# The next group's filter work spread over two superblocks, and its square root moved from ScalarE to three Newton steps on VectorE

## The chip, the cores and the metric

One core of a Trainium2 chip runs the whole program. The metric is the device time of one execution in microseconds (us); lower is better.

## What is computed

The input `x` is (8, 64, 56, 56) in float32. Four layers follow each other, each with its own group normalisation and a residual:

```
x = x + L0(gn(x))   # decoupled dynamic 3x3 filter
x = x + L1(gn(x))   # 1x1 convolution gated by a sigmoid
x = x + L2(gn(x))   # 3x3 convolution with ternary weights
x = x + L3(gn(x))   # attention over the 3136 pixels, softmax
```

The change touches what L0 needs before its taps. From the normalised image it makes two filters:

```
y  = relu(mean(x) @ w1.T + b1) @ w2.T + b2          # 9 taps per channel
cf = (y - mean) / (std(ddof=1) + 1e-10) * fn_std     # channel filter
sf = einsum(x, ws) + bs                              # 9 taps per pixel
sf = (sf - mean) / (std(ddof=1) + 1e-10) * gain      # spatial filter
out = sum over taps of patch * cf * sf
```

The standard deviation of `sf` needs one square root per pixel.

## The kernel before

**Groups and layers.** Two images make a group on the 128 partitions (64 channels each); there are 4 groups, three in a loop and the last written out after it. A group goes through L0, L1, L2 and L3 in order. A chunk is 448 pixels (8 rows), 7 chunks to an image.

**Attention.** L3 takes the queries in 7 superblocks of 448 columns, and the keys in 25 steps of 128 rows. In step j TensorE (PE) waits for the exponentials of step j (`exp_done`), multiplies them with the values (L1239, 4 matmuls), and makes the scores of step j+2 (L1195, 4 matmuls). ScalarE (ACT) takes the exponential of the scores of a step (L897) into one of 5 buffers, once GpSimd (POOL) has added the buffer of five steps before into its running sum (L1008). Superblocks 0 to 5 also find the maxima of the next superblock: 49 tiles, about two a step, made by PE (L1163) in PSUM banks 4, 5 and 7 in rotation and reduced by VectorE (DVE, L665); three rows of blocks of them are summed by ACT too (L854), two steps later. The tiles for the last superblock end at step 19 of superblock 5 (`SPLIT_STEP`), after which DVE splits the maxima (`split_max`) and PE and ACT move them into the query rows (L1188, L869). Superblock 6, the last, has no such tiles. A superblock's denominators (L1205, L1209) come at step 2 of the next one, the reciprocals (L701 to L705) on DVE at step 3, and POOL's two products of `finish` (L987, L989) after its step 8; after the last superblock they follow at once.

**The front.** What the next group's L0 needs before its taps is called the front. It reads `xin`, which the queue of SyncE has loaded again at the start of L3, and no DMA belongs to it. In groups 0 to 2 it is spread over the steps of superblock 6 by one function `front_at(j)` per engine; for group 0 it runs at the start of the program (the prologue), with no attention beside it. Its parts, by step:

- DVE: the statistics of the 7 chunks (`front_stats`, L468) at step 0, `squares` at 3, `var_eps` at 4, `front_bias` at 6, `front_mid` at 8, `front_sum_squares` (L538 to L542) at 15, `front_parts` (L546 to L562) at 18, `front_centre` (L514 to L523) at 19, `front_channel_filter` (L525 to L529) at 22.
- PE: the pair mean and pair variance (L1038, L1042) at 2 and 3, the small product of `front_mid` (L1047) at 7, the spatial filter (L1060, 8 matmuls for each of 7 chunks) at 8 to 14, the channel filter (L1052, 18 matmuls) at 16, and the transposes of the split filter (L1071) at 20, 20, 21, 22, 23, 24, 24.
- ACT: the normalisation of a chunk (L777) at 7 to 13, the square root (`front_root`, L795) after the exponential of step 16, and a copy of each transposed piece (L799) one step after its transpose, the last two behind the superblock.
- POOL: `power` (L954) before its step 5 and `channel_root` (L958) before its step 21.

Every engine takes its instructions in the order of the program, so a wait in one of these parts also holds what is behind it. `link` makes DVE wait for its own last result before the next instruction. The first tap of the next group (L1085) waits for all 7 copies, and the PE transposes wait for `front_parts`. The last denominators on PE wait for POOL's last sum.

`plan_banks` gives the maximum tiles, the max rows and the denominators their PSUM banks by estimated times. The front uses banks 4 and 5 (`FB`, `SFB`).

The square root and what follows it:

```python
nc.scalar.activation(sfs[:, 4, :], sfs[:, 2, :], ACT.Sqrt, scale=1.0 / (TAPS - 1))
# front_parts: one Newton step on it
s0 = s4 + 1e-30;  s1 = 1 / s0
s3 = (s2 * 0.5/(TAPS-1)) * s1
s5 = s4 * 0.5 + s3
```

Of the kernel before, what the change touches and what calls it, by code (L numbers as in the profile page):

```python
# [13 lines left out]
F32R = mybir.dt.float32r  # L14
BF16 = mybir.dt.bfloat16
# [11 lines left out]
NJ = HW // CH  # L27
# [29 lines left out]
FRONT_XN = 7  # L57
FRONT_SF = 8
FRONT_TR = (20, 20, 21, 22, 23, 24, 24)
FRONT_ROOT = 16  # L60
# [34 lines left out]
def plan_banks():  # L95

    tiles, rows, dens = {}, {}, {}
# [20 lines left out]
    for k in range(NQ * (NJ - 1)):  # L118
# [14 lines left out]
    return tiles, rows, dens  # L133


TILES_AT, ROWS_BANK, DEN_BANK = plan_banks()


# [30 lines left out]
def build(nc, x, weights, vectors, cst, out):  # L169
    with ExitStack() as ctx:  # L170
# [129 lines left out]
        sfvar_ready = sem("sfvar_ready")  # L300
        sfsd_ready = sem("sfsd_ready")
# [57 lines left out]
        FRONT_LINKS, LINKS = 23, 31  # L359
# [67 lines left out]
        def _(dve):  # L427
# [70 lines left out]
            def front_stats(g):  # L498
                n[0] = 0
                dve.wait_ge(x_loaded, 16 * g + 16)  # L500
                for i in range(NJ - 1):
                    chunk_stats(xin, i)
                mean_var(g, 0, chunk_stats(xin, NJ - 1))
# [32 lines left out]
            def front_sum_squares(g):  # L536
# [28 lines left out]
            def group(g, more):  # L565
# [142 lines left out]
                def front_at(j):  # L708

                    if j == 0:  # L710
# [666 lines left out]
```

## Time and profile before

| what | value |
|---|---|
| median of 3 runs | 1879.36 us (1878.1 to 1879.47) |
| the profiled execution | 1879.96 us |
| its span, first to last instruction | 1878.2 us |
| PE busy | 1646.5 us, 88% |
| DVE busy | 1258.0 us, 67% |
| ACT busy | 1249.8 us, 67% |
| POOL busy | 1099.3 us, 59% |

The span is from the first to the last instruction of the core; the execution is 1.76 us longer. A busy share is an average over stages with different limits. PE is the TensorE matmul and PEld its weight load. In a timeline row the first number is the start in us from the span's start, the second the time taken by all instructions of the row, `x` how many they are, and the bracket how long the engine had been idle before it and what ended that. An instruction that has started and has to wait for a port of the memory shows the wait in its duration.

### The profile page before, as it was taken

How to read it: one execution, taken by the hardware profiler on the slowest of the kernel's cores; microseconds unless marked ns; L12 is line 12 of the kernel's file. 1: busy time of each engine (PE TensorE's matmuls, PEld its weight loads, DVE VectorE, ACT ScalarE, POOL GpSimd, SP SyncE). 2: the span in 40 equal slices, each digit the busy share in tenths (PEclk: the TensorE clock that was granted, in tenths of full speed). 3: DMA queues.
4: the chain of work that ended last, by engine and by line, in shares of the span. 5: the costliest groups of instructions: out<-in, count | busy, mean ns of one | idle time of the engine just before them, and what ended most of it. 6: DMA issues, size and time to landing. Idle time of an engine off the chain costs nothing.

```text
span 1878.2 us, 35981 instructions
## 1 busy us (share of the span) xinstructions
PE 1646.5 (88%) x10840; PEld 826.0 (44%) x10840; DVE 1258.0 (67%) x2446; ACT 1249.8 (67%) x2324; POOL 1099.3 (59%) x898
## 2 busy tenths in 40 slices
PE   5887899999887699999988779999999787999997
PEld 4363344444436344444444534444454353444442
DVE  5947777775584777777467477777748657777760
ACT  2036788888412788888831278888872347888885
POOL 3610577778651067777855006777777402677777
PEclk9988899999889899999998889999999898999998
DMA  2004000000000400000000040000000011000000
GB/s 84 0 1 86 2 7 6 6 6 7 11 0 1 86 1 6 6 6 7 11 7 1 1 85 1 6 6 11 6 6 6 0 27 26 6 6 6 6 6 11
DMA packets 10104, 26.91 MB, mean 14 GB/s; under 512 B 2256, under 2 KB 6608, under 8 KB 9424
## 3 DMA queue, kind: packets, MB, share of 16 engines
q1 hardware_dynamic: 9936, 24.79, 5.5%
q8 instruction: 90, 1.47, 0.3%
q14 instruction: 78, 0.64, 0.1%
HBM read 8.73 MB, written 6.42 MB: 8 GB/s over the span
## 4 chain that ended last, share of the span: by engine, by line
PE 54%; issue 15%; DVE 12%; POOL 9%; ACT 9%; POOLq 1%; DVEq 0%; ACTq 0%
PE PS L1239 22%; PE PS L1163 11%; PE PS L1195 10%; DVE nmt L672 4%; ACT PS L854 3%; DVE nmt L665 2%; ACT Pb L897 2%; PE PS L1060 2%; POOL VT L970 2%; POOL VT L965 2%; PE PS L1135 2%; POOL VT L967 2%; POOL VT L974 1%; POOL accP L1008 1%; PE PS L1126 1%
## 5 line engine op out<-in xcount | busy, mean ns | idle before, releaser
L665 DVE TENSOR_REDUCE nmt<-PS 128x1 f32<-128x448 f32 x1176 | 680.3, 620 | 280.8 <-PE PS L1163 276.4
L1008 POOL TENSOR_TENSOR accP<-accP,Pb 128x512 f32<-128x512 f32 (+1 forms) x532 | 678.3, 1275 | 168.1 <-ACT Pb L897 144.6
L897 ACT ACTIVATE Pb<-PS 128x896 f32<-128x896 f32 (+1 forms) x700 | 638.9, 914 | 130.2 <-PE PS L1195 107.9
L1239 PE MATMUL PS<-Pb,VT 128*64 128x448 f32 x2800 | 656.0, 548 | 4.4 <-ACT Pb L897 3.6
L1163 PE MATMUL PS<-Ka,Qa 96*64 96x448 bf16 x2744 | 480.9, 362 | 55.9 <-DVE nmt L665 28.1
L1195 PE MATMUL PS<-Qa,Ka 99*64 99x448 bf16 x2744 | 489.8, 358 | 5.3 <-ACT Qa L869 4.0
L854 ACT ACTIVATE PS<-PS,nmt 128x448 f32<-128x448 f32 x588 | 356.3, 606 | 56.8 <-DVE nmt L672 29.4
L1163 PEld LDWEIGHTS PS<-Ka,Qa 96*64 96x64 bf16 x2744 | 159.4, 111 | 324.3 <-issue 127.2
L1195 PEld LDWEIGHTS PS<-Qa,Ka 99*64 99x64 bf16 x2744 | 162.3, 111 | 248.8 <-issue 184.3
L1239 PEld LDWEIGHTS PS<-Pb,VT 128*64 128x64 f32 x2800 | 191.6, 138 | 96.2 <-ACT Pb L897 24.5
L777 ACT ACTIVATE xnp<-xw,nb,rstd 128x448 f32<-128x448 f32 x56 | 40.5, 750 | 204.9 <-DVE nb L487 204.9
L1001 POOL TENSOR_TENSOR accQ<-Pb 128x512 f32<-128x512 f32 x28 | 35.6, 1271 | 234.2 <-ACT Pb L897 234.2
L579 DVE SCALAR_TENSOR_TENSOR Pb<-PS,cf,xnp 128x448 f32<-128x448 f32 x252 | 154.9, 677 | 17.1 <-PE PS L1085 13.4
L1093 PE MATMUL PS<-Pb,cs 128*128 128x448 f32 x280 | 135.5, 566 | 0.7 <-DVE Pb L579 0.7
L1008 POOL TENSOR_TENSOR accQ<-accQ,Pb 128x512 f32<-128x512 f32 x84 | 106.7, 1270 | 46.2 <-ACT Pb L897 44.9
L854 ACT ACTIVATION_READ_ACCUMULATOR PS<-PS,nmt 128x1 f32 x588 | 116.0, 197 | 0.0
L954 POOL TENSOR_TENSOR rstd<-ve,mhalf 128x1 f32<-128x1 f32 x16 | 8.8, 550 | 172.0 <-DVE ve L483 172.0
L672 DVE TENSOR_REDUCE nmt<-PS 128x1 f32<-128x448 f32 x196 | 104.8, 613 | 1.7 <-PE PS L1163 1.7
L1085 PE MATMUL PS<-xnf,selb 96*128 (+1 forms) x252 | 84.9, 376 | 13.3 <-issue 6.2
L777 ACT ACTIVATE xnf<-xw,nb,rstd 128x448 f32<-128x448 f32 x28 | 20.7, 752 | 102.8 <-DVE nb L487 102.8
L1135 PE MATMUL PS<-xh,wt 128*128 (+1 forms) x252 | 64.3, 404 | 10.6 <-ACT xh L777 10.6
L1085 PEld LDWEIGHTS PS<-xnf,selb 96*128 96x128 bf16 x252 | 25.0, 99 | 90.5 <-DVE Pb L579 50.7
(141 smaller groups left out, 1435.0 us busy)
## 6 DMA issues: line engine op xcount, KB each, us to landing
xin<-in_x SPq DMA_DIRECT2D x4, 1568.0 KB, 12.2
out<-xw SPq DMA_DIRECT2D x28, 224.0 KB, 1.9
Qa<-parts SPq DMA_DIRECT2D x24, 168.0 KB, 6.9
Ka<-parts SPq DMA_DIRECT2D x24, 112.0 KB, 3.8
Ka<-parts SPq DMA_DIRECT2D x24, 84.0 KB, 2.6
wz<-in_weights SPq DMA_DIRECT2D x1, 829.0 KB, 8.2
Qa<-parts SPq DMA_DIRECT2D x24, 28.0 KB, 1.9
cs<-in_cst SPq DMA_DIRECT2D x1, 576.0 KB, 8.8
```

Of the source, the lines that this page charges most:

```text
L579: nc.vector.scalar_tensor_tensor(out=rows(prod[:, t, :]), in0=rows(PS[:, t % TAP_BANKS, 0:CH]), scalar=cf[:, t:t + 1], in1=pad_rows_at(xnp ...
L665: nc.vector.reduce_max(nmt[:, target % 2, b, t:t + 1], PS[0:BLK, bank, 0:CH], X, negate=True).then_inc(mx_free, 1)
L672: nc.vector.reduce_max(nmt[:, 0, b, t:t + 1], PS[0:BLK, i % NJ, 0:CH], X, negate=True).then_inc(first_used, 1)
L854: return nc.scalar.activation(PS[0:BLK, bank, 0:CH], PS[0:BLK, bank, 0:CH], ACT.Exp, bias=nmt[:, target % 2, b, t:t + 1], accum_out=sm[:, ...
L897: nc.scalar.activation(Pb[0:r, j % PSLOTS, :, :], PS[0:r, 2 * (k % 2):2 * (k % 2) + 2, 0:CH], ACT.Exp).then_inc(exp_done, 1)
L1008: nc.gpsimd.tensor_tensor((accQ if j < TO_ACCP else accP)[0:r, :, REST:CH], (accQ if j <= TO_ACCP else accP)[0:r, :, REST:CH], Pb[0:r, j % ...
L1085: mm(PS[:, t % TAP_BANKS, 0:CH], selb[:, t, :], SF[:, ds(j * CH, CH)], start=True, stop=True).then_inc(tap_ready, 1)
L1093: mm(PS[:, ACCB + odd, 0:CH], identf, prod[:, t, :], start=(t == 0), stop=(t == TAPS - 1)).then_inc(tap_added, 1)
L1135: last = mm(PS[:, j, 0:CH], wt[:, t * P:(t + 1) * P], pad_rows_at(src, j * (ROWS * PW) + (t // 3) * PW + t % 3, ROWS), start=(src is xh an ...
L1163: last = mm(PS[C * h:C * h + C, bank, 0:CH], Qa[0:KROWS, h, s * CH + b * C:s * CH + b * C + C], Ka[0:KROWS, h, t * CH:(t + 1) * CH], start ...
L1195: ins = mm(PS[c:c + C, 2 * (k % 2) + h, 0:CH], Ka[0:KROWS + 3, h, j * QC + c:j * QC + c + C], Qa[0:KROWS + 3, h, s * CH:(s + 1) * CH], sta ...
L1239: last = mm(PS[C * h:C * h + C, OB, 0:CH], VT[:, j, C * h:C * h + C], Pb[:, j % PSLOTS, h, :], start=(j == 0), stop=(j == NQ - 1))
```

## The change

The front starts in superblock 5: its steps are now counted from the start of superblock 6, with negative ones in superblock 5. DVE takes one chunk of the statistics in each of the steps -17 to -11 (steps 8 to 14 of superblock 5) ahead of that step's maximum tiles. The pair mean, squares and pair variance come at -5 and -4, POOL's power at -3, the normalisations at -1 to 5, the spatial filter at 1 to 7, `front_sum_squares` at 8, the root at 10, `front_centre` at 11, `front_parts` at 12, the channel filter at 9 (PE), 14 (POOL) and 16 (DVE), and the transposes at 19, 19, 20, 21, 22, 23, 23. In DVE's order `front_centre` now stands ahead of `front_parts`. The square root is a seed from the bits of the variance and three Newton steps on DVE, and ACT's `Sqrt` is gone; the scaling by 1/(TAPS-1) is in the squares. The prologue uses the same functions.

```diff
-FRONT_XN = 7
-FRONT_SF = 8
-FRONT_TR = (20, 20, 21, 22, 23, 24, 24)
-FRONT_ROOT = 16
+FRONT_STATS = -17
+ROOT_BITS = float(0x1FBD1DF5)
+FRONT_MEAN = -5
+FRONT_XN = -1
+FRONT_SF = 1
+FRONT_TR = (19, 19, 20, 21, 22, 23, 23)
...
-        bank = min(free, key=lambda b: free[b][0])
+        bank = min((b for b in free if b not in front), key=lambda b: free[b][0])
...
+        if k == NQ * (NJ - 1) + FRONT_MEAN:
+            front = {b: free[b][1:] for b in (4, 5)}
...
-                link(g, nc.vector.tensor_tensor(sf2[:, :, :], sf[:, :, :], sf[:, :, :], ALU.mult))
-                nc.vector.reduce_sum(sfs[:, 2, :], sf2[:, :, :], X).then_inc(sfvar_ready, 1)
+                link(g, nc.vector.scalar_tensor_tensor(out=sf2[:, :, :], in0=sf[:, :, :], scalar=1.0 / (TAPS - 1),
+                                                       in1=sf[:, :, :], op0=ALU.mult, op1=ALU.mult))
+                link(g, nc.vector.reduce_sum(sfs[:, 2, :], sf2[:, :, :], X))
+
+            def front_root(g):
+                link(g, nc.vector.tensor_scalar(sfs[:, 4, :].bitcast(I32), sfs[:, 2, :].bitcast(I32), 0.5, ROOT_BITS,
+                                                ALU.mult, ALU.add))
+                for old, new in ((4, 5), (5, 4), (4, 5)):
+                    link(g, nc.vector.reciprocal(sfs[:, 1, :], sfs[:, old, :]))
+                    link(g, nc.vector.scalar_tensor_tensor(out=sfs[:, 3, :], in0=sfs[:, 2, :], scalar=0.5,
+                                                           in1=sfs[:, 1, :], op0=ALU.mult, op1=ALU.mult))
+                    link(g, nc.vector.scalar_tensor_tensor(out=sfs[:, new, :], in0=sfs[:, old, :], scalar=0.5,
+                                                           in1=sfs[:, 3, :], op0=ALU.mult, op1=ALU.add))
...
             def front_parts(g):
-                dve.wait_ge(sfsd_ready, g + 1)
-                link(g, nc.vector.tensor_scalar(sfs[:, 0, :], sfs[:, 4, :], 1e-30, None, ALU.add))
-                link(g, nc.vector.reciprocal(sfs[:, 1, :], sfs[:, 0, :]))
-                link(g, nc.vector.scalar_tensor_tensor(out=sfs[:, 3, :], in0=sfs[:, 2, :], scalar=0.5 / (TAPS - 1),
-                                                       in1=sfs[:, 1, :], op0=ALU.mult, op1=ALU.mult))
-                link(g, nc.vector.scalar_tensor_tensor(out=sfs[:, 5, :], in0=sfs[:, 4, :], scalar=0.5,
-                                                       in1=sfs[:, 3, :], op0=ALU.mult, op1=ALU.add))
...
-            def front_root(g):
-                act.wait_ge(sfvar_ready, g + 1)
-                nc.scalar.activation(sfs[:, 4, :], sfs[:, 2, :], ACT.Sqrt, scale=1.0 / (TAPS - 1)).then_inc(sfsd_ready, 1)
...
-                        if s == NJ - 1 and more:
-                            front_at(j)
+                        if s >= NJ - 2 and more:
+                            front_at(j - NQ * (NJ - 1 - s))
...
-                with pool.Fori(1, NJ - 1) as s:
+                with pool.Fori(1, NJ - 2) as s:
                     superblock(NJ * g + s, s, False)
-                superblock(NJ * g + NJ - 1, NJ - 1, False, more)
+                superblock(NJ * g + NJ - 2, NJ - 2, False, -NQ if more else None)
+                superblock(NJ * g + NJ - 1, NJ - 1, False, 0 if more else None)
...
-                    if j == 2:
+                    if j == FRONT_MEAN:
+                        wait_bank(FRONT_LAST[FB])
                         pair_mean(g + 1, 0, front)
```

## Rows read from the trace of the kernel before

**Rows 1.** The page: the chain that ended last, shares of the span

```profile
PE 54%; issue 15%; DVE 12%; POOL 9%; ACT 9%; POOLq 1%; DVEq 0%; ACTq 0%
```

**Rows 2.** Windows (start:end length, busy us by engine, granted clock, DMA): last superblock, groups 0, 1

```profile
450.55:499.52 48.97, 47.79 (x345) 23.75 (x342) 18.08 (x40) 34.90 (x48) 36.73 (x30) 0.97 0.02 6
913.08:962.46 49.38, 46.23 (x345) 23.24 (x342) 18.62 (x40) 34.95 (x48) 36.60 (x30) 1.00 0.02 6
```

**Rows 3.** Timeline of ACT, superblock 6 of group 0

```profile
461.90 0.92 ACT L897 ACTIVATE Pb<-PS 128x896 f32<-128x896 f32 x1 [0.30 <-PE PS L1195]
...
463.37 0.91 ACT L897 ACTIVATE Pb<-PS 128x896 f32<-128x896 f32 x1
...
476.79 0.92 ACT L897 ACTIVATE Pb<-PS 128x896 f32<-128x896 f32 x1 [1.28 <-PE PS L1195]
478.99 0.92 ACT L897 ACTIVATE Pb<-PS 128x896 f32<-128x896 f32 x1 [1.28 <-PE PS L1195]
479.93 1.28 ACT L795 ACT_TABLE_LOAD   x1
...
482.90 1.28 ACT L897 ACT_TABLE_LOAD   x1
```

**Rows 4.** Windows: the stretch of group 0 behind that

```profile
486.00:488.00 2.00, 2.00 (x10) 0.68 (x8) 1.97 (x2) 0.43 (x1) 1.92 (x2) 0.50 0.00 0
```

**Rows 5.** Timeline of ACT, superblock 6 of group 3, which has no front

```profile
1843.64 0.92 ACT L897 ACTIVATE Pb<-PS 128x896 f32<-128x896 f32 x1 [0.31 <-PE PS L1195]
...
1846.01 0.92 ACT L897 ACTIVATE Pb<-PS 128x896 f32<-128x896 f32 x1 [0.31 <-PE PS L1195]
```

**Rows 6.** Groups by line and shape on PE, 440 to 500 us: busy us, mean ns

```profile
L1052 PE MATMUL PS<-y,wz 24*128 24x1 f32 x18 | 2.2, 246 | 0.0
L1209 PE MATMUL PS<-accP,ones 128*64 128x256 f32 x8 | 1.2, 380 | 0.0
L1205 PE MATMUL PS<-cs,dcol 128*64 128x64 f32 x24 | 1.1, 225 | 0.0
```

**Rows 7.** Timeline of DVE, the prologue

```profile
29.22 0.68 DVE L538 TENSOR_TENSOR sf<-PS,vec 116x504 f32<-116x504 f32 x1 [9.13 <-PE PS L1060]
...
30.65 0.68 DVE L542 TENSOR_REDUCE sfs<-sf 116x56 f32<-116x504 f32 x1
...
31.87 0.50 DVE L548 RECIPROCAL sfs<-sfs 116x56 f32<-116x56 f32 x1
...
32.91 0.19 DVE L553 TENSOR_SCALAR sfs<-sfs 116x56 f32<-116x56 f32 x1
...
34.40 0.42 DVE L559 CAST sfp<-sf 116x504 bf16<-116x504 f32 x1
...
36.03 0.69 DVE L562 TENSOR_TENSOR sfp<-sf,sfp 116x504 bf16<-116x504 f32 x1
...
37.88 0.15 DVE L522 TENSOR_SCALAR ys<-ys 128x1 f32<-128x1 f32 x1
...
39.09 0.23 DVE L529 SCALAR_TENSOR_TENSOR cf<-yf,ys,vec 128x9 f32<-128x9 f32 x1
```

**Rows 8.** Timeline of DVE, superblock 5 and the start of 6, group 0

```profile
434.44 1.16 DVE L665 TENSOR_REDUCE nmt<-PS 128x1 f32<-128x448 f32 x2 [0.36 <-PE PS L1163]
...
447.99 3.79 DVE L468 BATCH_NORM_STATS2 st<-xin 128x6 f32<-128x448 f32 x7
```

**Rows 9.** Timeline of DVE, superblock 6 of group 1

```profile
948.42 1.38 DVE L559 CAST sfp<-sf 116x504 bf16<-116x504 f32 x1
...
956.91 0.85 DVE L529 SCALAR_TENSOR_TENSOR cf<-yf,ys,vec 128x9 f32<-128x9 f32 x1
```

**Rows 10.** Timeline of POOL, superblock 6 of group 0

```profile
468.27 6.67 POOL L1008 TENSOR_TENSOR accP<-accP,Pb 128x512 f32<-128x512 f32 x5
```

**Rows 11.** Timeline of POOL, superblock 6 of group 1

```profile
947.80 6.20 POOL L1008 TENSOR_TENSOR accP<-accP,Pb 128x512 f32<-128x512 f32 x4 [3.92 <-ACT Pb L897]
```

**Rows 12.** Timeline of PE, superblock 6 of group 1

```profile
954.60 0.61 PE L1071 MATMUL PS<-identb,sfp 116*96 116x116 bf16 x8 [1.97 <-DVE sfp L562]
```

More of the change, by code:

```diff
@@ L14 @@
 F32R = mybir.dt.float32r
+I32 = mybir.dt.int32
 BF16 = mybir.dt.bfloat16
@@ L95, in plan_banks @@
 def plan_banks():
-    tiles, rows, dens = {}, {}, {}
+    tiles, rows, dens, front = {}, {}, {}, {}
     free = {4: (0.0, "nothing", 0), 5: (0.0, "nothing", 0), 7: (0.0, "nothing", 0)}
     def take(at, lasts, what, count):
-        bank = min(free, key=lambda b: free[b][0])
+        bank = min((b for b in free if b not in front), key=lambda b: free[b][0])
         last = free[bank][1:]
@@ L130, in plan_banks @@
             dens[s - 1] = take(k + 0.8, 1.5, "transposed", 2 * (s - 1) + 1)
+        if k == NQ * (NJ - 1) + FRONT_MEAN:
+            front = {b: free[b][1:] for b in (4, 5)}
         if j == ROWS_STEP:
             rows[s + 1] = take(k + 0.8, 2.5, "rows", s + 2)
-    return tiles, rows, dens
-TILES_AT, ROWS_BANK, DEN_BANK = plan_banks()
+    return tiles, rows, dens, front
+TILES_AT, ROWS_BANK, DEN_BANK, FRONT_LAST = plan_banks()
 COLS = {}
@@ L357, in build @@
         stored = sem("stored")
-        FRONT_LINKS, LINKS = 23, 31
+        FRONT_LINKS, LINKS = 30, 38
         block = ctx.enter_context(nc.Block())
@@ L494, in stats, with front_stats @@
                 bias(g, layer, small)
[L498 to L501, printed above, removed]
+            def front_stats(g, i):
+                if i == 0:
+                    n[0] = 0
+                    dve.wait_ge(x_loaded, 16 * g + 16)
+                if i < NJ - 1:
                     chunk_stats(xin, i)
-                mean_var(g, 0, chunk_stats(xin, NJ - 1))
+                else:
+                    mean_var(g, 0, chunk_stats(xin, NJ - 1))
             def front_bias(g):
@@ L753, in group @@
                 reciprocals(NJ * g + NJ - 1, 7)
-            front_stats(0)
+            for i in range(NJ):
+                front_stats(0, i)
             centre_weights()
@@ L762, in _ @@
             front_sum_squares(0)
+            front_root(0)
             front_parts(0)
@@ L883, in front_at @@
                             front_spatial_filter(g + 1, i)
-                    if j == FRONT_ROOT:
-                        front_root(g + 1)
                 def superblock(s):
@@ L909, in superblock @@
                             max_rows(sidx + 1, s + 1, ROWS_BANK[s + 1][0])
-                        if s == NJ - 1 and more:
-                            front_at(j)
+                        if s >= NJ - 2 and more:
+                            front_at(j - NQ * (NJ - 1 - s))
                 load_table(ACT.Exp)
@@ L923, in group @@
                     superblock(s)
-                if more:
-                    for j in range(NJ):
-                        if FRONT_TR[j] == NQ - 1:
-                            front_spatial_filter(g + 1, j)
                 copy_output(NJ * g + NJ - 1)
@@ L931, in _ @@
                 front_normalise(0, j)
-            front_root(0)
             for j in range(NJ):
@@ L990, in finish, with front_at, superblock @@
                                             ALU.add).then_inc(fin_done, 1)
-                def superblock(sidx, s, first, front=False):
+                def front_at(j):
+                    if j == FRONT_MEAN + 2:
+                        power(g + 1, 0)
+                    elif j == FRONT_SF + NJ + 6:
+                        channel_root(g + 1)
+                def superblock(sidx, s, first, front=None):
                     for j in range(1, NQ):
-                        if front and j == 5:
-                            power(g + 1, 0)
-                        if front and j == 21:
-                            channel_root(g + 1)
+                        if front is not None:
+                            front_at(j + front)
                         r = key_rows(j)
@@ L1263, in superblock @@
                             denominators(sidx - 1, bank)
-                        if s == NJ - 1 and more:
-                            front_at(j)
+                        if s >= NJ - 2 and more:
+                            front_at(j - NQ * (NJ - 1 - s))
                         if j == ROWS_STEP and s < NJ - 1:
```

33 lines of the change are left out of this document (17 added, 16 removed).

## The prediction

> **What bounds the kernel now.** I read the chain of waits first: more than half of the span hangs on PE [rows 1]. Then the windows of superblock 6, the only place besides the prologue where the front runs: from the exponential of step 24 of superblock 5 to the end of the last denominators, group 0 takes 48.97 us and group 1 49.38 us [rows 2]; group 2 takes what group 0 does. In 48.97 us PE is busy for 47.79, and DVE for 18.08. So this stretch is PE's: DVE has room in all, but PE waits for it in places. The timelines show where.
>
> A plain step is paced by PE: in group 3 two steps take 2.37 us, so 1.18 each [rows 5]. A step with a chunk of the spatial filter takes 2.20 us [rows 3], so a chunk costs PE 1.02. A normalisation beside an exponential makes ACT's step 1.47 [rows 3]. After the exponential of step 16 ACT loads a table, waits for the variances, takes the root and loads the exponential's table again: it is back at 484.18, 4.3 us after 479.91 [rows 3]. PE fills part of that with the channel filter (2.2 us [rows 6]), then runs dry, and behind it the granted clock is 0.50 for 2 us, the 1.2 GHz level [rows 4]. Group 1 shows no such fall (1.00 [rows 2]) and loses its time elsewhere: PE waits 1.97 us for `front_parts` before the first transposes [rows 12]. A stall here is thus partly exchanged for another, which matters below.
>
> **The change, part by part.** The base is the profiled execution, 1879.96 us (span 1878.2 and 1.76 around it), 0.6 above the median of the runs, 1879.36. I call no change what lies within 0.2%, 3.8 us, about what a measurement of this kernel can tell.
>
> *Prologue, nothing hides it.* From the end of the reduction (30.65 + 0.68 = 31.33) to L553 at 32.91 the old root with its one Newton step takes 1.58 us [rows 7]. The new one is a seed like L553 (0.19 and a gap, 0.22) and three rounds of one reciprocal and two products; L548 to L553 is one such round, 1.04 us [rows 7]. That is 3.34, so **+1.8 us**. The variances' square keeps its size. PE, ACT and the taps all wait for this chain.
>
> *Statistics in superblock 5.* At steps 8 to 14 DVE reduces two tiles in 1.16 us and is idle for 0.36 [rows 8], a step of 1.52 with PE without a gap. A chunk of statistics costs 3.79/7 = 0.54 [rows 8]. Each step is overdrawn by 0.18, over seven steps 1.3 us. The banks let DVE be late by about its idle time, 0.36; the rest PE waits for in its bank waits, with scores and values queued behind. **+0.9 us** a group, ends 0 (all absorbed) and 1.3. Before, these 3.79 us lay in DVE's empty time.
>
> *Pairs.* Mean and variance go from steps 2 and 3 of superblock 6 to 20 and 21 of superblock 5, ahead of the max rows. Their four PE passes, by the 2.2 us for 18 [rows 6], make 0.5; part of it lies beside ACT. I book 0.4 ahead of the window and take them out of it. POOL's `power` waits for them, ahead of one sum; POOL's gaps at the turn of the superblock take that. SyncE's queue carries nothing of the front.
>
> *Superblock 6, PE's account in the new order*, from the exponential of step 24. ACT first: two exponentials with a normalisation (2 x 1.47), the output copy (0.5) and the exponential of step 1 (0.92) make 4.4 us until PE can start step 1. Then 19 plain steps (22.4), the small product (0.3), the denominators (half of 1.2 + 1.1, 1.15 [rows 6]), 7 chunks (7.1) and the channel filter (2.2): PE reaches the first transposes at 37.6. From there on group 1 shows 954.60 to 962.46, 7.9 us [rows 12, 2]; one more step with its transpose, 1.5, comes on top, and the last pair of pieces no longer stands behind the last exponential, -0.4: 9.0. Without any wait the window ends at 46.6 + 0.4 = 47.0, that is **2.0 us less** than 48.97. POOL, at 1.33 us a sum (6.67/5 [rows 10]) from its `finish` on, would end within 0.5 us of that. All of ACT's 4.3 us stall is gone in this number, with the low clock behind it.
>
> *Does DVE's chain keep up?* It begins when the last chunk is done: 4.4 + 7 x 1.18 + 0.3 + 1.15 + 7.1 = 21.2. PE then needs 37.6 - 21.2 = 16.4 us to the transposes. With POOL silent, the prologue gives the chain's length: L538 to the end of L562, 36.72 - 29.22 = 7.5; the Newton rounds +1.8; `front_centre`, now ahead of `front_parts`, 36.72 to 38.03, 1.3: 10.6 [rows 7]. But POOL isn't silent. The cast L559 takes 0.42 in the prologue and 1.38 beside POOL's sums, and the small L529, a product of two tensors, 0.23 and 0.85 [rows 7, 9]: 0.6 to 0.96 more for each. POOL pays too, 1.55 a sum and not 1.33 [rows 11, 10]. This is what the Trainium skill says (SBUF — State Buffer, "Who interferes with whom"): a DVE instruction in a two-port mode or with two SBUF inputs excludes a POOL instruction that reads SBUF, for the whole of it. By that rule both products of a Newton round are exposed and the reciprocal is not, and the trace agrees for L529.
>
> The old chain did its Newton step in the 3.92 us that POOL was idle through ACT's stall [rows 11]. With the stall gone, that cover is gone: the root now runs beside a POOL that works without a break. The added wait: the four long operations of `front_parts` 3.8 (0.96 each); the square, the seed and L519 about 1.7 together; each round 0.4 to 0.5, since the reciprocal lies beside a sum and the two products fit together between two sums; and half of 0.96 for L555. Together 7.4, so the chain takes 18.0 us, ends 14.4 (only the four long ones wait) and 26 (all sixteen exposed operations wait 0.96). POOL's `channel_root` waits for `front_centre`, which now stands behind the rounds; about 1 us of POOL, with later sums queued behind it.
>
> So PE waits 18.0 - 16.4 = **1.6 us** at step 19. Window 48.6; POOL, slowed by the exclusions and the root, adds 0.5 at the denominators: 49.1, against 48.97, 49.38 and 48.97. Sum over three groups: 0.0. What goes at ACT comes back at DVE and POOL.
>
> Total: 1.8 + 3 x 0.9 + 0.0 = **+4.5 us**, 1884.5 profiled, 1883.9 as a median; 0.24%.
>
> **The rivals.**
>
> *A. DVE keeps up: not slower.* Place: PE's first transposes at step 19; it decides if the chain takes 16.4 us or less. For it: where POOL waits for an exponential, DVE's products go through free, and the window has such gaps around the channel filter. Against it: group 1's transposes waited for `front_parts` although only four operations met POOL. The price: 47.0 x 3 against 147.3, -6.3; with +1.8 and 2.7 for the statistics, -1.8 (1877.6); if the banks absorb the statistics too, -4.5 (1874.9).
>
> *B. DVE is much later, and the clock falls.* If every product of the rounds waits for a sum of its own, six times 0.96 in place of 1.4 in all, the chain grows by 4.4 us; or PE's wait brings the 0.50 clock as behind the wait in group 0 [rows 4], 2 to 3 us at half speed, 1 to 1.5 lost. One of these in each group gives +4 to +13 on the forecast, 1888 to 1897; the lower half is likelier, as POOL is then held back too and frees DVE. For it: two of three groups show the fall now. Against it: group 1 waited longer and kept 1.00.
>
> *C. The change does not take the stall away.* If some other function still loaded a table, 4.3 us would stay. The trace has exactly two loads around L795 and none around the copies and normalisations, so I give it nothing.
>
> **How the numbers follow.** Forecast (DVE a little late) 0.45, +1 to +8 us by the ends of the statistics and of the chain; rival A 0.33, -4.5 to 0; rival B 0.22. Slower by over 0.2%: 0.6 of the forecast and nearly all of B, 0.48. Faster by over 0.2%: 0.4 of A, 0.14. The rest, 0.38. The likeliest case alone reaches from 1880.5 to 1887.5. The range leaves out the best corner of A and the upper half of B: 1876.0 to 1890.5.
>
> **What would show it.** In the changed profile: no table load inside superblock 6; DVE without idle time before L665 at steps 8 to 14 of superblock 5 and PE waiting for L665 there, up to 0.9 us in all; products of the Newton rounds that take about 1 us in the groups and 0.22 in the prologue; an idle time of PE before the first L1071, ended by L562; POOL waiting for L522 ahead of L958; the first tap of group 0 1.8 us later. I am wrong if PE does not wait at L1071 (then A), or if superblock 5 keeps its 1.52 us steps; the window of superblock 6 is the number that decides, 49.1 against 47.0.

## The result and the profile after

The changed kernel takes 1888.80 us in the median of five runs (1886.76 to 1889.99), the kernel before 1879.36 (1877.99 to 1880.94): a ratio of 1.0050, 95% interval 1.0036 to 1.0065, so 0.5% slower. Between the two profiled executions, span against span, it is 1885.0 against 1878.2, +6.8 us. The one of the changed kernel is the quickest of its five, 2.0 under their median, and the one of the kernel before 0.6 over its own, so the ledger below is short of the medians' +9.4 by 2.6.

Where the 6.8 us are:

| piece | before | after | difference |
|---|---|---|---|
| prologue and layers, to the exponential of step 24 of superblock 0, group 0 | 238.31 | 238.43 | +0.1 |
| superblock 5, groups 0, 1, 2 | 41.48, 41.47, 41.47 | 42.53, 42.54, 42.53 | +3.2 |
| window of superblock 6, groups 0, 1, 2 | 48.97, 49.38, 48.97 | 50.90, 50.90, 50.90 | +5.4 |
| from there to the exponential of step 24 of the next superblock 0 | 201.36, 200.64, 195.77 | 200.10, 200.02, 195.63 | -2.0 |

The rest, 0.1, lies in group 3. The first and the last piece differ from one profiled execution to the next where the code is the same: e3 and e4 below have the changed kernel's code there, and show 240.24 and 239.61 for its 238.43 in the first, and 597.4 and 598.3 for its 595.8 in the three of the last. So neither the +0.1 nor the -2.0 can be put down to the change. The windows do repeat, within 0.05 us from group to group and in e3. Each window, as before, runs from the exponential of step 24 of superblock 5 to the end of the last denominators. Windows of the changed kernel, group 0: the whole one (it answers to [rows 2]) and two short stretches behind the wait. Columns are start:end, length, busy us (and instructions) of PE, PEld, DVE, ACT and POOL, granted clock, DMA share, GB/s.

```profile
451.70:502.60 50.90, 47.17 (x341) 23.08 (x337) 22.20 (x37) 32.36 (x45) 37.40 (x30) 0.97 0.02 6
492.00:494.00 2.00, 1.88 (x12) 0.95 (x14) 1.14 (x4) 1.44 (x3) 1.92 (x2) 0.63 0.00 0
494.00:496.00 2.00, 2.00 (x12) 0.90 (x10) 0.00 (x0) 0.52 (x2) 1.79 (x2) 0.52 0.03 8
```

DVE is busy for 22.2 us and not 18.1, although the new root adds only 1.8 us of work and 3.8 us of statistics have left. The timeline of DVE says why; the same instructions stand first as the prologue has them, where POOL is silent, and then as superblock 6 of group 0 has them.

```profile
29.93 0.68 DVE L546 SCALAR_TENSOR_TENSOR sf<-sf 116x504 f32<-116x504 f32 x1
...
32.12 0.22 DVE L556 SCALAR_TENSOR_TENSOR sfs<-sfs 116x56 f32<-116x56 f32 x1
32.37 0.22 DVE L558 SCALAR_TENSOR_TENSOR sfs<-sfs 116x56 f32<-116x56 f32 x1
...
36.18 0.42 DVE L569 CAST sfp<-sf 116x504 bf16<-116x504 f32 x1
```

```profile
473.14 1.43 DVE L546 SCALAR_TENSOR_TENSOR sf<-sf 116x504 f32<-116x504 f32 x1
...
475.78 0.50 DVE L555 RECIPROCAL sfs<-sfs 116x56 f32<-116x56 f32 x1
476.32 0.79 DVE L556 SCALAR_TENSOR_TENSOR sfs<-sfs 116x56 f32<-116x56 f32 x1
477.14 1.31 DVE L558 SCALAR_TENSOR_TENSOR sfs<-sfs 116x56 f32<-116x56 f32 x1
...
480.07 0.64 DVE L556 SCALAR_TENSOR_TENSOR sfs<-sfs 116x56 f32<-116x56 f32 x1
480.75 1.32 DVE L558 SCALAR_TENSOR_TENSOR sfs<-sfs 116x56 f32<-116x56 f32 x1
...
485.95 1.38 DVE L569 CAST sfp<-sf 116x504 bf16<-116x504 f32 x1
...
490.44 1.62 DVE L572 TENSOR_TENSOR sfp<-sf,sfp 116x504 bf16<-116x504 f32 x1
```

A product of 56 columns takes 0.22 us in the prologue and up to 1.32 beside POOL's sums; a reciprocal, which reads one operand, 0.50 in both. In POOL's timeline of the same stretch the cost to the other side is seen: eight sums take 1.47 each, not 1.33 [rows 10], and the channel filter's root waits for `front_centre`.

```profile
483.59 0.55 POOL L961 TENSOR_TENSOR ys<-ys,phalf 128x1 f32<-128x1 f32 x1 [1.60 <-DVE ys L527]
484.10 11.77 POOL L1016 TENSOR_TENSOR accP<-accP,Pb 128x512 f32<-128x512 f32 x8
```

And PE's timeline shows who pays: PE has made its scores and stands for 3.04 us ahead of the first transposes, in all three groups. Before, only group 1 waited there, 1.97 [rows 12].

```profile
488.52 0.55 PE L1204 MATMUL PS<-Qa,Ka 99*64 99x448 bf16 x4
492.12 0.67 PE L1080 MATMUL PS<-identb,sfp 116*96 116x116 bf16 x8 [3.04 <-DVE sfp L572]
```

Right behind it the granted clock is 0.63 and then 0.52, mostly the 1.2 GHz level, where the ten us ahead of it (482 to 492) had 1.00.

In superblock 5 the statistics stand between the pairs of reductions, and DVE has no idle time left: its pairs follow each other every 1.59 us, against 1.52 [rows 8].

```profile
426.94 1.16 DVE L675 TENSOR_REDUCE nmt<-PS 128x1 f32<-128x448 f32 x2 [0.37 <-PE PS L1172]
428.01 0.62 DVE L471 BATCH_NORM_STATS2 st<-xin 128x6 f32<-128x448 f32 x1
428.54 1.14 DVE L675 TENSOR_REDUCE nmt<-PS 128x1 f32<-128x448 f32 x2
429.60 0.61 DVE L471 BATCH_NORM_STATS2 st<-xin 128x6 f32<-128x448 f32 x1
```

PE and ACT do not slow down in these steps: from the exponential of step 7 to that of step 14 both kernels take 10.88 us in group 0. The 1.05 us are lost later. The exponential of step 16 comes 1.93 us after the one before it, where it was 1.55: PE waits for a bank that ACT's sum of a maximum tile (L864) holds, and that sum had waited for DVE, which is behind by then. The exponentials of steps 23 and 24 come after 1.59 and 2.07 us, where it was 1.14 and 1.88: there the pair mean (L1047) and the pair variance (L1051) stand in PE's order, 0.38 us each. ACT's row, then PE's:

```profile
437.65 0.61 ACT L864 ACTIVATE PS<-PS,nmt 128x448 f32<-128x448 f32 x1 [0.39 <-DVE nmt L675]
```

```profile
438.43 0.38 PE L1172 MATMUL PS<-Ka,Qa 96*64 96x448 bf16 x2 [0.45 <-ACT PS L864]
...
447.84 0.38 PE L1047 MATMUL PS<-mv,cs 128*128 128x1 f32 x2
...
449.44 0.38 PE L1051 MATMUL PS<-sq,cs 128*128 128x1 f32 x2
```

### The profile page after: what moved, and what is told of

It is laid out like the page before. It is cut to its first block, busy times and chain, and to the rows that moved or that the text cites. A ratio compares the mean times of both kernels' runs of the same rounds, so it can differ in the third digit from the quotient of the medians.

```text
span 1885.0 us, 35918 instructions
## 1 busy us (share of the span) xinstructions
PE 1643.7 (87%) x10840; PEld 823.2 (44%) x10840; DVE 1278.4 (68%) x2470; ACT 1240.8 (66%) x2313; POOL 1099.3 (58%) x898
## 3 DMA queue, kind: packets, MB, share of 16 engines
q8 instruction: 90, 1.47, 0.3%
## 4 chain that ended last, share of the span: by engine, by line
PE 51%; issue 15%; DVE 15%; POOL 10%; ACT 8%; POOLq 1%; DVEq 0%; ACTq 0%
PE PS L1250 21%; PE PS L1172 11%; PE PS L1204 10%; DVE nmt L682 4%; ACT PS L864 3%; DVE nmt L675 3%; ACT Pb L905 2%; POOL accP L1016 2%; PE PS L1069 2%; PE PS L1144 2%; POOL VT L968 2%; POOL VT L973 2%; POOL VT L970 2%; POOL VT L977 1%; PE PS L1135 1%
## 5 line engine op out<-in xcount | busy, mean ns | idle before, releaser
L864 ACT ACTIVATE PS<-PS,nmt 128x448 f32<-128x448 f32 x588 | 356.2, 606 | 57.7 <-DVE nmt L682 28.2
L864 ACT ACTIVATION_READ_ACCUMULATOR PS<-PS,nmt 128x1 f32 x588 | 115.9, 197 | 0.0
L1094 PE MATMUL PS<-xnf,selb 96*128 (+1 forms) x252 | 84.0, 372 | 13.5 <-issue 6.6
L711 DVE STREAM_TRANSPOSE Rr<-PS 128x448 f32<-128x448 f32 x28 | 18.0, 643 | 77.8 <-PE PS L1218 77.8
```

What stands on the lines that cost most here:

```text
L864: return nc.scalar.activation(PS[0:BLK, bank, 0:CH], PS[0:BLK, bank, 0:CH], ACT.Exp, bias=nmt[:, target % 2, b, t:t + 1], accum_out=sm[:, ...
L1094: mm(PS[:, t % TAP_BANKS, 0:CH], selb[:, t, :], SF[:, ds(j * CH, CH)], start=True, stop=True).then_inc(tap_ready, 1)
```

## The experiments

All windows are those defined above, for groups 0, 1, 2. The first four runs share a median of the kernel before of 1878.52 us, the next four one of 1878.32, the last two one of 1878.57. In brackets behind a time stand the recorded ratio to the kernel before and its 95% interval; the ratio lies up to 0.0007 above the quotient of the two medians. Windows and waits are those of one profiled execution of each version, and these also differ from each other in stages whose code is the same, as the first piece of the table shows.

### 1. The root back on ScalarE, the front early (e1)

```
-    for old, new in ((4, 5), (5, 4), (4, 5)):
+    act.wait_ge(sfvar_ready, g + 1)
+    nc.scalar.activation(sfs[:, 4, :], sfs[:, 2, :], ACT.Sqrt).then_inc(sfsd_ready, 1)
```

on ScalarE behind the exponential of step 10, with one Newton step on DVE as in the kernel before.

> The changed kernel with the square root given back to ACT (after its exponential of step 10) and one Newton step on DVE; the front stays early. Theory (DVE's chain beside POOL is what PE waits for): the chain from L543 to the end of the last split falls from 19.6 us to about 15, below the 16.6 us that PE needs, so no wait before the first transposes and no low clock; ACT's stall of about 3 us at step 10 lies beside PE's channel filter. Window of superblock 6 (exponential of step 24 to the end of the denominators) 46.5 to 47.5 us where the changed kernel has 50.9; time 1875 to 1879. Rival (the early place itself costs, by ACT's load at steps 0 to 2): the window stays at 49.5 or more, time 1884 or more.

Measured: 1882.09 us (1.0026, 1.0016 to 1.0036); windows 49.07, 48.60, 50.16. The wait at the transposes is gone, but the time isn't. ACT's timeline, with its own 4.1 us from the first table load to the next exponential:

```profile
470.94 1.28 ACT L810 ACT_TABLE_LOAD   x1
473.47 0.25 ACT L810 ACTIVATE sfs<-sfs 116x56 f32<-116x56 f32 x1 [1.25 <-DVE sfs L550]
473.74 1.28 ACT L912 ACT_TABLE_LOAD   x1
475.03 1.73 ACT L912 ACTIVATE Pb<-PS 128x896 f32<-128x896 f32 x2
```

Two windows of this run, 10 us each behind the stall, in groups 0 and 2:

```profile
475.00:485.00 10.00, 9.04 (x51) 3.53 (x52) 9.18 (x15) 6.33 (x8) 7.79 (x7) 0.83 0.00 2
1402.00:1412.00 10.00, 9.06 (x42) 3.38 (x44) 9.16 (x17) 5.37 (x6) 7.10 (x6) 0.66 0.00 1
```

My theory had the old stall of ACT covered once the front lay earlier, with windows of 46.5 to 47.5. It isn't. In groups 0 and 2 PE waits 0.95 us for the exponential and then works at a lower clock. In group 1 the clock stays at 1.00, and the window is still 48.60: behind the same 0.95, PE waits 1.31 us at the last denominators for POOL's last sum.

```profile
961.56 0.65 PE L1226 MATMUL PS<-accP,ones 128*64 128x256 f32 x4 [1.31 <-POOL accP L1024]
```

Of the changed kernel's loss this version keeps superblock 5 (42.53) and avoids some 1.6 us a window.

### 2. The Newton steps alone, the front where it was (e2)

```
-    nc.scalar.activation(sfs[:, 4, :], sfs[:, 2, :], ACT.Sqrt, ...)
+    for old, new in ((4, 5), (5, 4), (4, 5)):
```

with the changed kernel's `front_root` at step 16 on DVE.

> The kernel before with only the square root changed to three Newton steps on DVE; the front stays in superblock 6. Theory: without ACT's stall POOL is busy beside the whole chain, which takes about 17.5 us from L538 on where it took 11.2; PE waits about 7 us before the first transposes; window of superblock 6 53 to 55.5 us where it was 48.97; time 1890 to 1900. Rival (the length of the chain hardly matters, other places bound): window at most 50, time at most 1883.

Measured: 1887.20 us (1.0051, 1.0034 to 1.0067); windows 52.09, 53.44, 50.55; superblock 5 is 41.47, as before. The wait at the transposes, in PE's timeline of group 0:

```profile
495.59 0.61 PE L1071 MATMUL PS<-identb,sfp 116*96 116x116 bf16 x8 [4.19 <-DVE sfp L566]
```

Only the direction of the theory holds; wait, windows and time all lie under its sizes. The chain took 13.5 us (13.3 in group 2) and not 17.5, since POOL ran out of work once PE stood still, and the last four long operations then took 0.42 and 0.68. Without the earlier start the root on DVE costs 1.6 to 4.1 us a window. In group 2 the wait is shorter, as PE comes later to the transposes by a fall of its clock (0.50 from 1418 to 1420 us):

```profile
1425.57 0.61 PE L1071 MATMUL PS<-identb,sfp 116*96 116x116 bf16 x8 [2.55 <-DVE sfp L566]
```

The early front alone (e1) thus costs 0.26% and the Newton steps alone 0.51%; both together, the changed kernel, 0.50%. The early start takes back in the windows about what it costs in superblock 5, and the root on DVE loses with it or without it.

### 3. Superblock 5 without the statistics (e3)

In groups 1 to 3 the first six chunks' statistics are left out, so the mean and variance rest on old ones and the result is not that of the program.

```
                 if i < NJ - 1:
-                    chunk_stats(xin, i)
+                    if isinstance(g, int):
+                        chunk_stats(xin, i)
```

> The changed kernel without the statistics of the first six chunks in groups 1 to 3 (left out of the computation; the seventh and the rest stay). Theory (DVE is overdrawn at steps 8 to 14 of superblock 5): superblock 5, between the exponentials of step 24, falls from 42.53 to 41.9 us, three times 0.65, time 2 us below the changed kernel; superblock 6 keeps 50.9. Rival (the pairs ahead of the max rows are the whole rise of 1.05): superblock 5 stays at 42.5.

Measured: superblock 5 takes 42.12 in each group, 0.41 less than 42.53, windows 50.95; 1888.41 us (two runs; 1.0055, 1.0035 to 1.0075), which can't be told from the changed kernel. DVE's timeline shows the idle time of before back between the reductions:

```profile
430.22 1.16 DVE L676 TENSOR_REDUCE nmt<-PS 128x1 f32<-128x448 f32 x2 [0.36 <-PE PS L1173]
431.74 1.15 DVE L676 TENSOR_REDUCE nmt<-PS 128x1 f32<-128x448 f32 x2 [0.36 <-PE PS L1173]
```

So the six chunks cost 0.41 a group, under half of what I had put on them: the exponential of step 16 is back at 1.54 us. The other 0.65 stays, and the trace places it: the exponentials of steps 23 and 24 still come after 1.59 and 2.07, where the pairs stand.

### 4. The transposes two steps later (e4)

```
-FRONT_TR = (19, 19, 20, 21, 22, 23, 23)
+FRONT_TR = (21, 21, 22, 22, 23, 23, 24)
```

and the last copy on ScalarE stands behind the superblock.

> The changed kernel with the transposes two steps later, at 21, 21, 22, 22, 23, 23, 24. Theory: PE needs 2.4 us more to get there and waits 0.7 us in place of 3.0, and the clock stays high; more copies stand at the end. Window of superblock 6 48.3 to 49.5 us where it was 50.9, time 1882 to 1885. Rival (POOL's backlog, not the wait, sets the end): window 50.4 or more.

Measured: 1884.33 us (1.0034, 1.0020 to 1.0048); windows 48.95, 48.77, 48.94. In groups 0 and 2 PE now waits 0.65 at the transposes, and 1.96 somewhere else:

```profile
493.28 0.61 PE L1082 MATMUL PS<-identb,sfp 116*96 116x116 bf16 x8 [0.65 <-DVE sfp L572]
...
501.12 0.65 PE L1220 MATMUL PS<-accP,ones 128*64 128x256 f32 x4 [1.96 <-POOL accP L1018]
```

POOL's timeline has the reason, eleven sums without a gap at 1.44:

```profile
485.22 15.84 POOL L1018 TENSOR_TENSOR accP<-accP,Pb 128x512 f32<-128x512 f32 x11
```

In group 1, where the clock falls for a while behind the channel filter, the two waits are 0 and 0.81. Two us of the window come back, as expected. A wait moved out of the way shows POOL's backlog right behind it: the contention costs twice, in DVE's chain and in POOL's sums.

### 5. and 6. Operands of the front in PSUM (e5, e6)

Banks 4 and 5 are the front's own there. In e5 the temporaries of the Newton steps, the reciprocal of the deviations, the scaled taps and the first residue lie in them:

```
+sfq = PS[0:SP2, SFB, 0:504]; sf2q = PS[0:SP2, FB, 8:512]; half_step = two slots of 56 columns in FB
-reciprocal(sfs[:, 1, :], ...);  scalar_tensor_tensor(out=sfs[:, 3, :], ..., in1=sfs[:, 1, :], ...)
+reciprocal(half_step[0], ...);  scalar_tensor_tensor(out=half_step[1], ..., in1=half_step[0], ...)
-scalar_tensor_tensor(out=sf, in0=sf, ..., in1=per_pixel(3), ...);  sfv, sf2v = views of sf, sf2
+scalar_tensor_tensor(out=sfq, in0=sf, ..., in1=per_pixel(), ...);  sfv, sf2v = views of sfq, sf2q
```

and e6 has only the two temporaries.

> The changed kernel with the vector engine's front operands spread over both memories: the two temporaries of each Newton step, the reciprocal of the deviations, the scaled taps and the first residue lie in PSUM (banks 4 and 5, which are free there), so that no operation of the root or of the parts reads two operands from SBUF; the square alone still does. Theory (operations with two SBUF operands wait for the end of a sum on the GpSimd engine and hold it off; those with one in PSUM don't): both products of a round 0.22 us each whatever GpSimd does, the chain from the square to the last part 12 to 13.5 us instead of 19.6, no wait ahead of the first transposes, the sums of GpSimd below the chain at 1.35 instead of 1.47, the windows 47.3 to 48.5 instead of 50.90, the time 1877 to 1882. Rival (what costs is the number of linked operations, whose waits are there whatever memory they read): the chain stays over 16 us, windows over 50, the time over 1885.

> The changed kernel with only the two temporaries of the Newton steps in PSUM; the parts are made from SBUF as they were. Theory (exclusion by two SBUF operands): the three rounds cost 0.94 each, the chain shrinks by 3.3 to 3.8 us to about 16, the wait ahead of the transposes falls from 3.04 to under 0.8, the parts keep their 7.7 us; windows 48.3 to 49.5, profiled time 1880 to 1884. Rival (the rounds wait for something else than the operand ports): rounds as before at 2.3 to 2.6 where GpSimd sums, chain over 18.5, windows over 50.3.

Measured, e5: 1878.11 us (0.9998, 0.9986 to 1.0009), windows 46.38, 46.37, 46.37, no wait ahead of the transposes. DVE's timeline of group 0:

```profile
478.40 0.22 DVE L560 SCALAR_TENSOR_TENSOR PS<-sfs,PS 116x56 f32<-116x56 f32 x1
478.65 0.21 DVE L562 SCALAR_TENSOR_TENSOR sfs<-sfs,PS 116x56 f32<-116x56 f32 x1
...
485.44 0.68 DVE L573 CAST sfp<-PS 116x504 bf16<-116x504 f32 x1
486.16 0.69 DVE L574 TENSOR_TENSOR PS<-PS,sfp 116x504 f32<-116x504 f32 x1
```

Chain: 474.50 to 488.28, 13.8 us for 19.6 (I expected 12 to 13.5, and windows from 47.3 up). In its prologue, where POOL is silent, the same products take 0.22 and 0.69 as well, so PSUM does not make them faster; it takes them out of POOL's way. The same products, the same links and waits, other memory: 0.22 and 0.69 where there were 0.79 to 1.32 and 1.62. The rival, that the number of linked operations is what costs, falls. Two more rows, of POOL (1.35 a sum) and of the window:

```profile
484.57 14.88 POOL L1020 TENSOR_TENSOR accP<-accP,Pb 128x512 f32<-128x512 f32 x11
```

```profile
453.77:500.15 46.38, 45.65 (x341) 22.64 (x337) 15.72 (x37) 32.36 (x45) 36.37 (x30) 1.00 0.02 7
```

e6: one profiled time, 1883.12 us; windows 47.89, 47.88, 48.46. Its three rounds take 1.04 each. In groups 0 and 1 its parts are as slow as in the changed kernel, the chain is 18.0 us, and the wait is 1.45, where I expected about 16 and under 0.8. So the rounds' share of the contention is worth 3.0 us of window there, 1.6 of wait and 1.4 of the clock behind it, and the parts' share another 1.5. Group 2 shows something else. The clock falls behind the channel filter, with PE busy all the time before and in it; the chain is 15.1 us, there is no wait at the transposes, and the window is longer all the same:

```profile
1404.00:1406.00 2.00, 2.00 (x10) 0.87 (x8) 1.76 (x8) 0.07 (x1) 0.99 (x1) 0.50 0.00 0
```

### 7. Two Newton steps instead of three (e7)

```
-for old, new in ((4, 5), (5, 4), (4, 5)):
+for old, new in ((4, 5), (5, 4)):
```

> The changed kernel with two Newton steps instead of three. Theory: the chain loses its third round, 2.0 to 2.6 us, and the wait ahead of the transposes falls from 3.04 to 0.5 to 1.1; the clock stays up or falls less behind it; windows 48.8 to 49.9, the time 1882 to 1885. Rival (the end of the window is set by the backlog of GpSimd, not by the wait of TensorE): the wait goes, the denominators wait for the sums instead, windows over 50.3, the time over 1886.

Measured: 1883.68 us (1.0031, 1.0019 to 1.0043); windows 47.90, 47.90, 47.91, wait 1.46. The chain lost 1.6 us, less than the 2.0 to 2.6 expected, and the wait is over the expected 0.5 to 1.1; yet the windows are 1 to 2 us shorter than I expected, and that tells what the wait really costs. PE's timeline, and the windows around it (those of the changed kernel stand above):

```profile
491.18 0.61 PE L1080 MATMUL PS<-identb,sfp 116*96 116x116 bf16 x8 [1.46 <-DVE sfp L572]
```

```profile
490.00:492.00 2.00, 0.82 (x10) 0.67 (x12) 1.93 (x4) 0.38 (x1) 1.92 (x2) 1.00 0.00 0
492.00:494.00 2.00, 1.95 (x16) 0.82 (x14) 0.28 (x1) 1.96 (x5) 1.84 (x3) 1.00 0.04 8
```

The wait shrank by 1.58 and the window by 3.00. Behind the wait this kernel needs 9.07 us (491.18 to 500.25) and the changed one 10.48 (492.12 to 502.60): 1.4 us less, at a granted clock of 1.00 where that one has 0.63 and 0.52. A wait of 1.46 left the clock up; behind one of 3.04 it fell.

The other runs bear this out. At the transposes twelve waits of 0.64 to 2.55 us (group 1 of before, group 2 of e2, and those of e4, e6, e7 and e8) have 1.00 over the 8 us behind them; the six of 3.04 to 3.06 (the changed kernel and e3) and the two of 4.2 (e2) have the fall behind them. Its price in window is 1.4 us, and 2.8 in group 1 of e2, where it lasts longer. But a long wait isn't the only thing that goes before a fall: in group 2 of e6, group 1 of e4 and group 2 of e2 the clock falls behind the channel filter, with PE busy throughout the eight us before. What decides those is open.

### 8. All together, and the statistics in DVE's empty steps (e8)

e5 and e7 in one, and

```
-FRONT_STATS, FRONT_MEAN, FRONT_XN, FRONT_SF = -17, -5, -1, 1
+FRONT_STATS, FRONT_MEAN, FRONT_XN, FRONT_SF = -5, -1, 3, 5
```

with the statistics two to a step.

> All that the runs point to, together: operands in PSUM as above, two Newton steps, the statistics of the next group two to a step at the steps 20 to 23 of superblock 5, where the vector engine has no maxima to make, and the front four steps later than in the changed kernel (spatial chunks at the steps 5 to 11 of superblock 6, three steps ahead of the kernel before), the transposes where they are. Theory: superblock 5 back at 41.5 to 41.7 instead of 42.53, the chain about 11 us from some 6.5 us later, so ready at about when TensorE comes to the transposes; windows 47.3 to 48.8; the time 1873 to 1878, the prologue's cost of the root included. Rival (what superblock 5 loses is in the plan of the banks or in the pairs of the mean and variance, not in the statistics): superblock 5 over 42.2, the time over 1880. Second rival (the window is set by the sums of GpSimd and can't fall under 49): windows 49 to 50, the time about 1880.

Measured: 1874.17 us (0.9982, 0.9973 to 0.9991), the lowest time of all versions (e9's interval overlaps it): 0.2% under the kernel before, and 0.7%, some 13 us, under the changed one (1.0050 against 0.9982). Superblock 5 takes 41.47, 41.48, 41.48: what it lost was the place of the statistics and of what followed them. The second rival falls. The first doesn't fall with this run, since the pairs and the reserved banks moved along with the statistics; the exponentials of steps 23 and 24 are back at 1.13 and 1.88, so for its 0.65 us the pairs are the cause, and for the 0.4 the statistics. DVE's timeline shows the seven chunks in one piece behind the last reductions, and the window of group 0:

```profile
447.55 3.79 DVE L471 BATCH_NORM_STATS2 st<-xin 128x6 f32<-128x448 f32 x7
```

```profile
450.10:497.19 47.09, 45.89 (x345) 23.54 (x342) 18.62 (x43) 32.49 (x45) 35.66 (x30) 1.00 0.02 7
```

### 9. The same, with the transposes a step later (e9)

```
-FRONT_TR = (19, 19, 20, 21, 22, 23, 23)
+FRONT_TR = (20, 20, 21, 22, 22, 23, 23)
```

> The last kernel (operands in PSUM, two Newton steps, the front four steps later) with the transposes at the steps 20, 20, 21, 22, 22, 23, 23 instead of 19, 19, 20, 21, 22, 23, 23, so that TensorE comes to them one step after the last part is written. Theory (each us of the wait that is left, 0.99, costs a us at the end): the wait goes, windows 46.0 to 46.5 instead of 47.09, the time 2 to 3 us below that kernel, 1870 to 1873. Rival (the transposes crowd the last steps and wait for their copies on ScalarE, or the sums of GpSimd end later than TensorE anyway): windows 46.9 to 48, no gain or a loss of up to 2 us.

Measured: the wait of 0.99 goes and the windows are 46.14 in all three groups, as the theory has it. But the time is 1875.62 us (0.9988, 0.9979 to 0.9998), not less than e8's. What the windows give (2.9 us in all) the other stages of the profiled execution take back: from a window's end to the exponential of step 24 of the next superblock 0 it is 202.52 and 202.43 in the first two groups, against 201.44 and 201.53 in e8 and 200.10 and 200.02 in the changed kernel. The windows from 10 to 20 us behind the last denominators, in which layer 0 makes its first taps, for e9, e7 and the changed kernel, in this order:

```profile
507.86:517.86 10.00, 9.85 (x29) 4.40 (x28) 8.21 (x14) 0.00 (x0) 6.78 (x7) 0.84 0.00 0
```

```profile
510.25:520.25 10.00, 9.85 (x29) 4.49 (x27) 8.13 (x14) 0.00 (x0) 6.52 (x6) 0.81 0.00 0
```

```profile
512.60:522.60 10.00, 9.84 (x33) 4.56 (x32) 9.66 (x17) 0.00 (x0) 6.26 (x6) 0.98 0.00 0
```

PE drops to the 1.2 GHz level in the gap at the turn of the group and comes back to 2.4 GHz at a varying time; here it comes back later and does four matmuls fewer in the stretch. What fixes that time isn't shown, nor that the shorter window has to do with it: the stretch up to the first superblock 0, which has the same code in e8 and e9 and lies ahead of every window, is 1.6 us longer in e9 as well. It was 1 to 3 us of scatter among my versions, and it is large enough to hide a gain of 1 us a group.

### 10. The kernel before, with its operands in PSUM (e10)

The edit of e5 in the kernel before, which keeps its root on ScalarE.

> The kernel before, with the square root on ScalarE and the front where it was, and only the operands of the front spread over SBUF and PSUM, as in the run that did so with the changed kernel. It says what the change is worth once the contention is gone, and whether the contention also bounded the kernel before. Theory (its parts lose 3 us, 485.9 to 491 becomes 485.8 to 488.6, the one wait of 1.97 in group 1 goes, but ScalarE's two table loads and its wait at the root stay in the middle of the superblock): windows 47.5 to 48.6, the time 1875 to 1878. Rival (the table loads cost nothing at the end of the window, and the contention was all there was): windows 46.3 to 47.0, the time 1871 to 1874, so that the change would be worth nothing even without the contention. Second rival (GpSimd's backlog sets the end of the window of before): windows 48.7 to 49.1, no difference.

Measured: 1876.95 us (0.9996, 0.9986 to 1.0005); windows 47.26, 48.95, 48.96. In group 0 the theory's 47.5 to 48.6 holds, a bit better; in the other two nothing is gained over 48.97 (0.4 over group 1's own 49.38), though no transposes wait. Their size is that of the second rival, but its reason isn't there: PE does not wait for POOL at the last denominators in any group. Two windows of 6 us behind ACT's stall, groups 0 and 1:

```profile
486.00:492.00 6.00, 5.16 (x37) 2.03 (x37) 5.43 (x12) 4.48 (x5) 4.69 (x4) 1.00 0.02 4
946.00:952.00 6.00, 5.94 (x28) 2.29 (x30) 5.01 (x13) 3.17 (x5) 4.37 (x4) 0.72 0.01 1
```

The clock again: 1.00 in the group that gained, 0.72 in the one that didn't, and the same behind the stall in group 2. PE's wait for the exponential is 0.84 us in all three, so what decides it isn't shown. Against e5's 46.37, which has no table load in the superblock, e10's windows are 0.9 us longer at the full clock and 2.6 where the clock falls. They also hold the pairs, 0.65 us, which e5 has ahead of its windows, so the root on ScalarE costs about 0.2 and 1.9 of that, an estimate from these rows. Had DVE and POOL not been in each other's way, the change was worth 6.1 us in the three windows, less 3.2 in superblock 5 and 1.8 in the prologue: some 1 us. The medians, 1878.11 for e5 and 1876.95 for e10, don't show even that; their intervals overlap.

## Why the prediction was right or wrong

The time measured, 1888.80, lies in the range, and slower was the likeliest side. But it lies above the 1880.5 to 1887.5 of the likeliest case, at the lower end of what rival B was given with a chance of 0.22. The forecast of 1883.9 was 4.9 us short. Its steps against the rows:

| step | predicted | measured |
|---|---|---|
| first tap of group 0 | +1.8 | +1.78 (43.70 for 41.92) |
| superblock 5, with 0.4 for the pairs | +1.3 | +1.05 |
| PE, from the last chunk to the transposes | 16.4 | 16.65 |
| DVE's chain | 18.0 | 19.64 |
| PE's wait | 1.6 | 3.04 |
| from there to the end | 9.0 | 10.48 |
| POOL at the denominators | +0.5 | 0 |
| window, without the pairs' 0.4 | 48.7 | 50.90 |

**What held.** The new order of PE's work: it came to the transposes 37.4 us into the window, with 37.6 predicted; without a wait the window was to end at 46.6, and e5 has 46.37. The place and cause of the new wait. No table load is left in superblock 6. The sign, and the greater part of its reason: what goes at ACT comes back in DVE's chain beside POOL, and 5.4 us more with it, where the forecast had the two even.

**The first term mis-sized: the exclusion in the Newton rounds.** Set against the prologue, operation by operation, DVE lost 9.0 us to POOL and not 7.4. The four long operations of `front_parts` lost 3.80 of the predicted 3.8, L565 1.05 for 0.48, the square and the seed 1.0 and L524 (L519 before) nothing, for 1.7 together, as POOL stood idle at L524. The three rounds lost 3.2 us where I had 0.4 to 0.5 each. My step was "the two products fit together between two sums". They don't: in rounds 1 and 3 the first product waits 0.6 or 0.4 and the second 1.1, for another sum; a sum of POOL starts between them. Only round 2 went free, while POOL stood idle for 0.98. The first condition of rival B came half true, then. The experiment with the temporaries in PSUM (e6) shows the size: 1.04 a round beside POOL's sums, as in the prologue.

This is the rule that the Trainium skill gives (SBUF — State Buffer, "Who interferes with whom"): a DVE instruction with two SBUF inputs shuts out a POOL instruction that reads SBUF, one with at most one SBUF input and outside the two-port modes doesn't. The trace agrees on both halves: beside the sums the same product takes 0.64 to 1.32 with both inputs in SBUF and 0.22 with one of them in PSUM (e5). In these rows it is DVE that waits.

**The second term mis-sized: what stands behind the wait.** I took 9.0 us from group 1 of before, whose wait of 1.97 left the clock at 1.00. Behind 3.04 it fell, 10.48. I had this as the other half of rival B and called it unlikely on the word of that one row; e7 confirms 9.07 at a wait of 1.46. With the fall each of these windows lost 1.4, 4.2 us in the three groups. All eight waits of 3 us and more have a fall behind them, and twelve shorter ones have none; as the clock also fell three times behind no wait at all, the wait as its cause is well borne out, but not proved.

**The rest.** The statistics were over-priced (0.41 for six of them against 0.9 for seven), the pairs under-priced (0.65 against 0.4); the sum was near. The place was wrong: I said that PE would wait for the reductions at steps 8 to 14 and that I was wrong if superblock 5 kept its 1.52 us steps. It kept them there, and PE paid at step 16 and at the pairs. The prologue's 1.8 us were there at the first tap and are 0.1 at the end of superblock 0, and the layers of the next groups are 2.0 us shorter: the clock of the first taps is not the same in any two versions. I had taken the stages outside for constant. Wait and clock, +6.6 (three windows of 50.90 for 48.7), and the layers, -2.0, with the prologue's -1.7 and superblock 5's -0.8, make 4.5 into 6.8 to within 0.2. So the profiled execution lies only 2.3 us over its forecast by luck: the windows alone were 6.6 off, and 3.7 of that is hidden by the scatter of the first taps. The other 2.6 us of the medians are the distance of the two profiled executions from them.

**The rivals.** A failed on its condition, the chain of 16.4 us. The version that meets it (e5) has windows of 46.37, and as a whole 1878.11, where A had 1877.6. B is what happened, in the lower part of its prices: two of the six products waited 1.1 us, most of a sum of their own, and two for part of one, and the clock fell in each group. C: no second pair of table loads.

## What to carry to other kernels

Before a step is moved from ScalarE to VectorE, ask which memory its operands lie in and whether GpSimd works at that time: small products of 0.22 us cost up to 1.32, as much as the sum beside them. Where a stretch of PSUM is free, one operand of each product and the source of each cast can lie there; it is worth what the chain is worth, about 10 us in the changed kernel and nothing that the runs can tell in the kernel before (0.9996, 0.9986 to 1.0005), where PE waited for the chain in one group only. A wait of TensorE is to be priced with the clock behind it: 1.5 us of wait were 1.5, 3 us were 4.4. And a difference of 1 to 3 us between two single profiled executions has to be looked for in stages that should be equal, too, before it is given to the change.

## What the runs showed of the hardware that was not expected

- The exclusion also met operations with one tensor operand: a TENSOR_SCALAR from SBUF to SBUF of 9 columns (L524) took 0.23 us in the changed kernel and 1.17 in e5, and the seed 0.19 in the prologue, 0.43 here and 0.95 in e8. When the products no longer waited, these did. The Trainium skill (VectorE: DVE Perf Modes, "Why PSUM operands drop a tier") has the other half: a PSUM operand rules out the mode that reads one tensor through both ports. The trace agrees: the cast takes 0.42 from SBUF and 0.68 from PSUM with POOL silent or not, but 1.38 from SBUF beside POOL. The slower form is the quicker one there.
- POOL paid with DVE: 1.47 a sum in the changed kernel, 1.44 in e4, 1.35 in e5.
- The clock at the start of the next group's taps moved between versions that don't differ there (0.81 to 0.98 over the same 10 us), and with it 1 to 3 us.
- The clock fell to 0.50 with TensorE busy for the whole stretch before, behind the channel filter (e6, group 2; e4, group 1; e2, group 2), and in most groups, with the same matmuls, it didn't fall there.
